# One-hot source lanes in 8 bits instead of 16, in a graph network kernel on one core

## The reference

```python
x = _layernorm(x + _L0_gnn_ref(x, edge_index, ...))   # one sum over neighbours, two dense layers
x = _layernorm(x + _L1_gnn_ref(x, edge_index, ...))   # four graph convolutions
x = _layernorm(x + _L2_gnn_ref(src, dst, x, edge_attr_64, ...))
x = _layernorm(x + _L3_gnn_ref(x, edge_index, ...))   # two mean aggregations
```

```python
in_deg = jax.ops.segment_sum(jnp.ones(src.shape[0]), dst, num_segments=N)
degs = in_deg + 1.0
norm = degs ** (-0.5)
edge_norm = (norm[src] * norm[dst])[:, None]
msg = edge_norm * (h[src] + e)          # e = efeat @ We + be
```

## Time and profile before

| What | Value |
|---|---|
| Median of 3 runs | 2571.49 us (2568.89 to 2573.13) |
| The profiled execution | 2577.17 us, of it a span of 2575.4 us |
| PE busy | 2471.7 us, 96% of the span |
| DVE busy | 1310.4 us, 51% |
| ACT busy | 599.5 us, 23% |
| In 577 to 838 us, with the lookups: PE, DVE | 258.45 and 203.86 of 261.00 us |
| There: granted PE clock, DMA share, bandwidth | 1.00, 0.72, 223 GB/s |

### The profile page before, as it was taken

The page is one execution under the profiler, slowest core; times in us unless marked ns, Lnnn a source line. Parts: engine busy times, 40 slices in busy tenths (PEclk is TensorE's granted clock), DMA queues, the critical chain, the costliest instruction groups (busy, mean ns, idle before and its releaser), DMA issues.

```text
span 2575.4 us, 38445 instructions
## 1 busy us (share of the span) xinstructions
PE 2471.7 (96%) x15593; PEld 1451.4 (56%) x15593; DVE 1310.4 (51%) x3605; ACT 599.5 (23%) x717; POOL 162.6 (6%) x117
## 2 busy tenths in 40 slices
PE   2889999899999999999999999999999999999998
PEld 1778899645555555555555555554445555555545
DVE  7887788467877666676656333332222122122222
ACT  3878999560000111111111000000000000000000
POOL 4000000010000111111111000000000200000000
PEclk9999999999999999999999999999999999999999
DMA  5736222346776666666666565545554554545553
GB/s 163 90 100 78 99 99 99 152 116 215 242 232 206 186 197 182 188 177 189 184 190 179 147 190 140 140 137 141 143 142 124 154 140 134 141 137 148 158 152 110
DMA packets 294910, 395.37 MB, mean 154 GB/s; under 512 B 82248, under 2 KB 282564, under 8 KB 291268
## 3 DMA queue, kind: packets, MB, share of 16 engines
q1 hardware_dynamic: 243960, 326.08, 45.7%
q10 hardware_dynamic: 49964, 64.80, 7.8%
q0 software_dynamic: 800, 1.94, 0.3%
HBM read 343.43 MB, written 49.32 MB: 153 GB/s over the span
## 4 chain that ended last, share of the span: by engine, by line
PE 89%; DVE 3%; DMA 2%; issue 2%; SPq 1%; ACT 1%; DVEq 1%; POOL 1%; ACTq 0%; POOLq 0%
PE PS L1709 83%; PE PS L1893 1%; SPq L530 1%; PE PS L1900 1%; PE PS L1901 1%; DVE TB L962 1%; PE PS L1915 1%; DMA edge_rows<-AT 1%; POOL AT L671 0%; PE PS L1845 0%; PE PS L1924 0%; PE PS L1895 0%; PE PS L1954 0%; DMA HR<-adjacency 0%; PE PS L1873 0%
## 5 line engine op out<-in xcount | busy, mean ns | idle before, releaser
L1709 PE MATMUL PS<-HR,HN 128*128 128x500 fp8e3 (+1 forms) x5096 | 1061.3, 365 | 1.9 <-DVE HN L1129 1.5
L1709 PE MATMUL PS<-HR,AGN 128*128 128x500 fp8e3 (+1 forms) x4606 | 917.9, 350 | 4.0 <-DMA HR<-adjacency 2.2
L1709 PEld LDWEIGHTS PS<-HR,HN 128*128 128x128 f16 x5096 | 489.0, 97 | 521.0 <-issue 9.5
L1709 PEld LDWEIGHTS PS<-HR,AGN 128*128 128x128 f16 x4606 | 446.6, 97 | 401.0 <-issue 3.0
L1709 PE MATMUL PS<-TB 128*128 128x245 f16 x1250 | 321.9, 277 | 28.5 <-DVE TB L962 20.3
L962 DVE TENSOR_TENSOR TB<-HN,HR 128x1240 f16<-128x1240 f16 x250 | 199.6, 798 | 0.0
L1206 DVE SCALAR_TENSOR_TENSOR AT<-PS,SC,TB 128x384 f32<-128x384 f32 (+24 forms) x50 | 21.6, 472 | 324.1 <-PE PS L1709 315.4
L1709 PEld LDWEIGHTS PS<-TB 128*128 128x128 f16 x1250 | 123.6, 100 | 54.3 <-DVE TB L962 13.2
L962 DVE TENSOR_TENSOR TB<-iot,HN 128x640 f16<-128x640 f16 x250 | 122.2, 489 | 62.6 <-PE PS L1709 61.9
L751 POOL TENSOR_TENSOR AT<-AT,dstI 128x1088 f32<-128x1088 f32 x49 | 100.2, 2045 | 740.8 <-DVE mxe L1332 740.8
L1359 DVE TENSOR_SCALAR TB<-iot,dstF 128x118 f16<-128x118 f16 (+1 forms) x833 | 142.0, 252 | 6.2 <-PE PS L1709 0.4
(11 more groups left out here) (248 smaller groups left out, 1672.9 us busy)
## 6 DMA issues: line engine op xcount, KB each, us to landing
HR<-adjacency SPq DMA_DIRECT2D x588, 437.5 KB, 3.5
AT<-source_lanes ACTq DMA_DIRECT2D x49, 544.0 KB, 4.9
AT<-in_edge_attr_dram ACTq DMA_DIRECT2D x144, 128.0 KB, 3.0
adjacency<-HN SPq DMA_DIRECT2D x9, 1531.2 KB, 5.7
adjacency<-HR SPq DMA_DIRECT2D x8, 1531.2 KB, 5.8
adjacency<-TB SPq DMA_DIRECT2D x8, 1531.2 KB, 5.5
HR<-adjacency SPq DMA_DIRECT2D x49, 218.8 KB, 2.5
AT<-in_edge_attr_dram ACTq DMA_DIRECT2D x48, 160.0 KB, 4.1
```

The lines of the kernel that those rows point to most:

```text
L1709: return t_.matmul(out_, w, m, start=start, stop=True, skip_group_check=True)
```

## The change

The one-hot `OHT` is kept in an 8-bit float (`float8e3`, the format of the adjacency) instead of a 16-bit one. It occupies the first half of the same place in `AT`. Its values are 0 and 1, exact in both. The input `BL` stays in 16 bits. The operation that writes it says `saturate=False`, which the 8-bit output type asks for. The matmul's other operand, the counts, stays in 16 bits. No instruction is added, removed or moved on any engine, and no wait is changed.

```diff
@@ -240,7 +240,7 @@
         BL = [AT[:, o + k * LW:o + (k + 1) * LW].bitcast(f16) for k in range(2)]
-        OHT = [AT[:, o + (2 + k) * LW:o + (3 + k) * LW].bitcast(f16) for k in range(2)]
+        OHT = [AT[:, o + (2 + k) * LW:o + (3 + k) * LW].bitcast(f8)[:, 0:J * P] for k in range(2)]
@@ -1310,7 +1310,7 @@
                 if g >= 2:
                     dve.wait_ge(s_lk, 2 * (g - 1))
-                v.tensor_scalar(OHT[g % 2], BL[g % 2], lane[:, 0:1], None, ALU.is_equal).then_inc(s_oht, 1)
+                v.tensor_scalar(OHT[g % 2], BL[g % 2], lane[:, 0:1], None, ALU.is_equal, saturate=False).then_inc(s_oht, 1)
```

## The result

The changed kernel takes 2577.06 us (median of 20 runs, 2573.11 to 2579.88) against 2571.41 us before (20 runs, 2567.07 to 2574.59). The ratio is 1.0021, with a 95% interval of 1.0015 to 1.0028: 5.6 us slower, 0.21%. The forecast was 2576.5 us.

A forecast was written before the change was run, and what follows sets the result against it. PE was taken to set the pace of the lookup stretch, with DVE having about a sixth of its time free. Tight places of 1.98 + 1.57 + 0.06 + 0.99 + 0.4 = 5.0 us on 2571.5 gave 2576.5 us, range 2569 to 2585.

The forecast's parts named there:

- The one-hot's length: DVE's 49 one-hots of 2176 elements: 1280 ns each instead of 785, 0.495 us more, 24 us of DVE time.
- The weight loads: PE's 833 loads, read as 8 bits instead of 16: taken as 0 change.
- The first groups: Start of the lookups, DVE without idle time: four one-hots all lengthen the path, 4 x 0.495 = 1.98 us.
- the very first one-hot: Runs beside POOL: lengthening covered by some 1.7 us until PE needs DVE; without cover 0.5 to 1.6 us.
- The two units with a lookup right behind the dense step: Two units 98 us apart: 0.495 us each, plus 0.29 two lookups further on; together 1.57 us.
- The places that just hold: Lookup with slack 0.93 us loses 0.06; three more, with 1.02, 1.11 and 1.15, just hold.
- The last unit: Lookups at 818.69 and 828.29 have no slack: 2 x 0.495 = 0.99 us.
- Behind the last group: DVE's split at 844.52, thought needed by PE's piece at 845.50, comes later: 0.4 us more.
- The sum: All tight places in the stretch with the lookups: 1.98 + 1.57 + 0.06 + 0.99 + 0.4 = 5.0 us slower.
- The rivals: DVE keeps rate: 2571.5 us, 0.05; one element a cycle: 2609, 0.05; loads slower: 2599, 0.06; faster: 2574, 0.04.
- What would show it: Profile signs: one-hot about 1280 ns, PE idle before lookups 2.1 to about 7 us, DVE's waits down some 20 us.
- the three large groups of the earlier trace: DVE's waits for PE and late lanes in the lookup stretch before the change, some 44 us in 260.

The follow-up runs named there:

- pe8: Kernel before with only PE's half changed: DVE writes 16-bit one-hots, PE reads the bytes as 8-bit weights; 2573.81 us, ratio 0.9999.
- after_again: The changed kernel profiled once more, for its trace; 2579.61 us in one run.
- dve8: Kernel before with only DVE's half changed: one-hot written in 8 bits, read by PE as 16-bit weights; 2579.11 us, ratio 1.0020.
- ahead8: Changed kernel with each one-hot made a turn earlier, behind the multiplications, and lanes asked for a turn earlier; 2573.13 us, ratio 1.0002.
- twice: Kernel before with each 16-bit one-hot written two times, a drain between; 2585.28 us, ratio 1.0037.
- halves8: Changed kernel with each 8-bit one-hot made by two instructions of 1088 elements; 2576.64 us in one run.
- ahead16: Kernel before with each 16-bit one-hot made a turn earlier, behind the multiplications, and lanes asked for a turn earlier; 2569.90 us, ratio 0.9989.
- halves16: Kernel before with each 16-bit one-hot made by two instructions of 1088 elements; 2574.31 us in one run.

## Why the prediction was right, and where it was not

The forecast was 5.0 us and the loss is 5.6; the mechanism is the one that was forecast: a one-hot at two elements in the time of four, which costs at the tight places alone. That the sum comes so near is in part luck, since terms that were too small and one with the wrong sign offset each other. By its steps:

- *The one-hot's length.* Forecast 1280 ns, measured 1348: 0.563 us more each instead of 0.495. The rate was right (0.522 ns against 0.514), the fixed part was mis-sized: I took over that of the 32-bit rows (294 - 256 x 0.514 = 162 ns), and this operation has 212, as it has 219 in 16 bits. The Trainium skill has the rule that an 8-bit stream keeps a one-source operation at two elements a cycle (DVE: opcode table, instruction layouts, handler registers and perf-mode slots, Perf-mode slots). No row of before showed it; the runs of after agree, 0.522 ns for an element against 0.260.
- *The weight loads.* Forecast 0, measured 0 (pe8). The Trainium skill (TensorE: Matmul & The Clock Gate, Weight-path perf modes) says that 8 bits run at the speed of 16, and also that the fast load reads more 8-bit weights at a time. The runs agree with the first (loads of 95 and 96 ns, 0.43 us from a lookup's start to the next piece in both); of the second nothing shows here, where the loads are all but hidden.
- *The first groups.* Forecast 1.98, measured 2.61 us (start of a lookup against its start before, both counted from lookup 0). Four times 0.563 are 2.25. The other 0.35 come from the very first one-hot, whose lengthening the prediction called covered. It runs beside POOL's seven additions (L719), which start 2.0 us apart but for one beside the one-hot, which takes 2.5 us before and 3.1 after. So they end 7.1 us into the stretch in place of 6.5, and the small DVE operation L1157, which stands ahead of the first groups, then ends only when they do. Before, and then after:

```profile
568.86 14.76 POOL L719 TENSOR_TENSOR XN<-XN,BR 128x896 f32 x7 [497.69 <-DVE HN L1129]
583.71 0.16 DVE L1157 SCALAR_TENSOR_TENSOR TB<-TB 128x1 f32<-128x1 f32 x1 [0.31 <-ACT TB L1547]
```

```profile
561.97 15.33 POOL L719 TENSOR_TENSOR XN<-XN,BR 128x896 f32 x7 [490.78 <-DVE HN L1129]
576.82 0.51 DVE L1157 SCALAR_TENSOR_TENSOR TB<-TB 128x1 f32<-128x1 f32 x1 [0.30 <-ACT TB L1547]
```

  POOL ends at 583.62 before, ahead of L1157, and at 577.30 after, 0.03 us ahead of L1157's end. In all six executions in which POOL still ran when this operation began (after, after_again, dve8, ahead8, twice, halves8) it took 0.42 to 0.51 us and ended within 0.03 us of POOL; in the other five POOL had ended and it took 0.16.
- *The two units with a lookup right behind the dense step.* Forecast 1.57, measured 1.02 + 1.03 us: 0.563 at each first place, 0.36 at each second, and 0.1 each because the loads of the lookup that waited, and so those of the next piece, start late.
- *The places that just hold.* Forecast 0.06 for one and 0 for three. Here the step failed: 1.10 us at the first, 0.26 at one of the three, 0.13 at another. Two one-hots in a row now add 1.13 us in place of 0.99, more than the slacks of 0.93, 1.02 and 1.11, and each lookup that has to wait costs 0.1 more. At the first place that makes 0.3 us; the other 0.8 come from the lanes' DMA that DVE waits for there. ACT's queue before (the first row), then after:

```profile
710.24 0.82 ACTq L1605 DMA_DIRECT2D AT<-source_lanes  x2
```

```profile
707.23 1.74 ACTq L1605 DMA_DIRECT2D AT<-source_lanes  x2
...
707.26 1.35 DVE L1313 TENSOR_SCALAR AT<-AT,lane 128x2176 fp8e3<-128x2176 f16 x1
...
712.88 1.35 DVE L1313 TENSOR_SCALAR AT<-AT,lane 128x2176 fp8e3<-128x2176 f16 x1 [1.46 <-DMA AT<-source_lanes]
```

  Counted from the start of the stretch, the first of the two DMAs is issued 3.9 us later than before, just as late as PE is there, so the prediction read this wait rightly. But it took 5.6 us to land in place of 4.8, and the one-hot at 712.88 starts when it has landed. (The second DMA waits for the one-hot at 707.26, whose buffer it fills, but it brings the lanes of the group after that.) These landing times differ between executions: in the second one of the changed kernel the same DMA took 4.8 us and the place cost 0.3 us, in dve8 3.9 us and nothing, and in the second execution another lanes' DMA, of group 7, took 5.4 us in place of 4.6 and cost 0.9. So about 0.8 us of the 6.1 are of this one execution's landing times and not of the mechanism.
- *The last unit.* Forecast 0.99, measured 1.13 us.
- *Behind the last group.* Forecast 0.4 us more, measured 1.2 us less: PE is 7.28 us late at the last lookup and 6.10 at the piece of the earlier trace rows. The reading of that row was wrong: the split at 844.52 was not what the piece needed, since after the piece starts at 844.71 and that split at 845.46. What held PE there was the adjacency's DMA, and it waited less: the waits for it ahead of the next pass's first two pieces are 0.78 and 1.42 us before, 0.71 and 0.31 after. The code agrees: that piece reads the node rows of an early unit. The distance of the two pieces is 4.3 to 4.7 us in the kernel before, pe8 and ahead16, and 3.3 to 3.9 in all the others, halves16 among them, whose DVE is hardly busier than before. The adjacency's DMA for the second piece took 6.7 us to land before and 5.5 after. The first loads of edge features (8 DMAs of 128 and 160 KB, ACT's queue) begin 1.0 us ahead of it before and 0.45 us after. Over all eleven executions the DMA took 5.3 to 5.8 us where the edge loads began 0.4 to 0.5 us ahead of it, and 5.9 to 6.8 where they began 0.9 us or more ahead. That fits a shared load on the DMA engines, but no run varied it alone, and this term stays open.
- *The sum.* 2.61 + 2.05 + 1.10 + 0.26 + 0.13 + 1.13 - 1.18 = 6.10 us in the stretch. The terms in front of the end came out 2.7 us above their forecast, most of it from the one-hot's fixed part and the places that just hold, and the end 1.6 us below.
- *The rivals.* DVE kept neither its rate (785 ns) nor fell to one element a cycle (2400); the loads were neither slower nor faster.
- *What would show it.* PE's waits before lookups were to rise to about 7 us at some nine places: 8.1 us at ten. DVE's waits were to shrink by some 20 us. Of the three large groups of the earlier trace rows, 43.8 us, two are left here with 18.2, and the third, L1324 for PE, is gone:

```profile
DVE TB L1224 <- PE PS L1893: 11.8, 5, 3.0
PE PS L1709 <- DVE TB L1324: 8.1, 10, 1.6
DVE AT L1313 <- DMA AT<-source_lanes: 6.4, 4, 1.9
```

  This is the view of after from 575 to 835 us. The wait for the very first lanes, 5.9 us, lies ahead of it there, since the stretch began earlier; with it 24.1 us are left, and the shrinkage is 19.7.

## What to carry to other kernels

A narrower type is no gain by itself: ask of each operation that writes or reads it whether its rate depends on the width, on each engine apart. Here it halved DVE's rate and left PE's as it was. When an engine with room on average gets a longer operation, list the slack at each point where the busy engine waits for it, and count how many of the longer operations lie in the chain since the engine last stood idle; treat slacks within a tenth or two of the added time as used up. And look at what stands in a chain without being needed by its end: with the one-hot behind the multiplications, and its lanes asked for earlier, the kernel with the slower one-hot is back at the time of before, although the first groups, where DVE never idles, still pay; the 16-bit kernel became a little faster than it was.

## What the runs showed of the hardware

DVE's comparison with a 16-bit input runs at 0.260 ns for an element when it writes 16 bits and at 0.522 ns when it writes an 8-bit float, with some 215 ns fixed in both. Weight loads of 128x128 take the same in 8 and in 16 bits (95 and 96 ns in the rows), and 17 pairs of load and matmul with 49 columns 0.43 us in both. A lookup that had to wait starts its loads late, and the following piece starts 0.52 us behind it instead of 0.43. A 1-element DVE operation that began while POOL's last addition ran took 0.42 to 0.51 us and ended with it, against 0.16 us behind it. The same DMA of lanes took between 3.9 and 5.6 us to land in four executions.
